# A transformer block's attention on one core: matmuls in column quarters and loop turns of one attention step

## The chip, the cores and the metric

The kernel runs on one core of one Trainium2 chip (trn2). The metric is the device time of one execution in microseconds. The time before is the median of three runs, 1502.8 us (1502.3 to 1504.57).

## What is computed

x has 2 batches of 2048 rows of 256 features, in float32. The block is a feed-forward layer, an attention and the same feed-forward layer again, each added to its input:

```
x = x + 0.5 * ffn(layernorm(x))
x = x + attention(layernorm(x))
x = x + 0.5 * ffn(layernorm(x))

ffn(x):        h = concat([x, -x]) @ K0        K: +1 or -1 by a boolean, 512x1024
               h = 2 relu(s0 h) @ K1           1024x1024
               h = 2 relu(s1 h) @ K2, times s2 1024x256
attention(x):  16 heads of 16 features, q = x wq + bq, k and v alike,
               softmax(q k^T / 4) v, heads side by side, @ wo^T + bo
```

## The kernel before, in words

**Blocks and layers.** The 4096 rows are worked in 8 blocks of 512 for each of the two feed-forwards: u = 0 to 7 is the first, 8 to 15 the second. A layer's output of 128 features for the 512 rows is one bank of PSUM (512 float32 in each of 128 partitions). The first layer (`l1`) and the second (`l2`) have 8 banks per block, the third (`l3`) 2, with rows on the partitions and two tiles of 256 columns in each bank. Activations are held as a float16 value and a float16 rest (`h_hi`, `h_lo`), so each product is made twice. Further kinds of bank are `qk` (q and k of a block), `v`, `out` (output projection) and `sq` (squares of q and k, for a bound on the scores).

**Attention.** There are 32 groups of 4 heads and 512 queries. A group has 8 steps, a step is two tiles of 128 keys. A step has four score pairs: each pair is two products of k with q, one on the lower and one on the upper 64 rows of the array, into two of the four score banks, and one ACTIVATE of ACT (L969) makes `exp` of both, 128x1024, into `prob`. Each tile of keys then has its products with v (`pe_values`, L898 to L915): 4 heads times 2 row halves, each a float32 matmul of 17 columns of weights, at columns 32 j of the array. Such a product stands as two MATMUL records in the trace. `pe_scores` (L880 to L895) makes a score either with all 128 columns of the array in one matmul for each row half, or, when `narrow` is set, as four matmuls of 32 columns (`columns_of`, L815): the same result, in four times as many instructions.

**Side work.** All other matmuls that fall into the time of attention are laid between its steps by a planner that writes one list of steps, `work`, before any instruction is made. Each engine goes through that list and issues its part of it. Side work is laid in pairs of banks (`lay_pair`, L259; `pe_pair`, L820 to L877): one bank on the lower 64 rows, its mate on the upper, and after half of its slots the two change rows, for which PE waits for the semaphore `halves`. A slot is one matmul for each bank, or four for each when `narrow` is set. A pair has 32 slots of 512 columns for `l2` (8 weight tiles, two terms, two row halves) and 8 for `l1`; 64 of 256 columns for `l3`; 4 (float32) for `qk`; 8 of 256 columns (float32) for `v` and `out`. `GAP` says how many slots are laid ahead of each score: 4 for `l1` and `l2`, 8 for `l3`, 1 for `qk`, 2 for `v` and `out`. The banks of a pair (6 and 7) are evicted by DVE and ACT: for `l1` and `l2` DVE makes both parts of one bank (L1007, L1009) and the rest part of the other, ACT (L942) the other's value. The next pair starts when they are free.

**The loop of turns** (L313 to L352). It runs over n = 1, 3, ... 255; one passage, here called a turn, issues the scores 4n to 4n + 7 and the products with v of the tiles 2(n-1) to 2(n-1) + 3, which belong to the steps n - 1 and n. At its head `lay_turn` (L291) lays what is not a pair: steps without matmuls (loads, fetches, `flip`), and long steps of DVE from the waiting list (`norm`, `xn`, `split`, `merge`, `heads`), all of them, or up to a cost of 1.0 where the next pair is of `l2`. If the head of the list `side` is of `l1`, the turn has two halves: two pairs of side slots and scores, then two products with v, each followed by a score; the second half has its side slots and scores in column quarters, the first half at full width. In every other turn four times (side slots, score) come first, all at full width, then four times (product with v, score in quarters). Scores laid behind a product with v are in quarters in every turn. `sq` and `range` are laid between the second and the third product with v (`lay_column`, L299), in such turns only. After the last turn of a group, step `o` lets DVE copy the group's output out of the two banks 4 and 5 (L1142, L1144) and SP store it with 8 DMAs; the next group's first product with v waits for that copy.

**DMAs.** At the first step of a group SP loads the k and q of the group after it (`sp_stage`, L1243 to L1262): 2 DMAs of 512 KB and 2 of 128 KB. It waits for the scores of the group before. SP also stores the output of each group, fetches attention rows, loads x and stores results. The engines' own instructions come over the queues named `instruction`; q8 carries those of PE.

Of the kernel before, what the change touches and what calls it, by code (L numbers as in the profile page):

```python
# [88 lines left out]
def build(nc, x, wq, bq, wk, bk, wv, bv, wo_t, bo, k0, k1, k2, s0, s1, s2, out):  # L89
# [29 lines left out]
    group_steps = key_tiles // 2  # L119
    att_steps = groups * group_steps  # L120
# [12 lines left out]
    def norm_turn(kind, u):  # L133
        steps = [Step("norm", u, kind), Step("xn", u, kind)]
        if kind == 1 or u:
            steps += [Step("split", u, kind), Step("flip", u, kind)]
        return steps

    def turns(kind, u):
        return [Step(kind, u, k) for k in range(kd)]  # L140
# [57 lines left out]
    side = norm_turn(0, 0) + [Step("w0", 0, 0)] + turns("turn_x", 0) + [Step("w0", 0, 1), Step("w0", 0, 2), Step("w1")]  # L198
# [3 lines left out]
    side = [s for s in side if s.kind != "load" or s.u < 2 * blocks]  # L202
# [11 lines left out]
    def lay(s, ring, on_act):  # L214
        s.on_act = on_act
        if s.kind in FILLS:
            numbers.lay(s, ring)
        find[s.kind, s.u, s.m] = s
        work.append(s)
# [10 lines left out]
    GAP = {"l1": 4, "l2": 4, "l3": 8, "qk": 1, "v": 2, "out": 2}  # L230
# [6 lines left out]
    def lay_idle(n):  # L237

        while side and side[0].kind not in GAP:
            s = side.pop(0)  # L240
            if s.kind == "fetch":
                held.append(s)
            elif s.kind in LONG:
                waiting.append(s)
            else:
                lay(s, SHARED, False)
        while held and n > group_steps * (block_groups * (held[0].u - blocks) + 2 * (held[0].m + 1)):
            lay(held.pop(0), SHARED, False)

    def lay_long(most):  # L250

        def unfetched(s):
            return s.kind == "heads" and any((f.u, f.m) <= (s.u, s.m // tpb) for f in held)

        while waiting and LONG[waiting[0].kind] <= most and not unfetched(waiting[0]):
            most -= LONG[waiting[0].kind]
            lay(waiting.pop(0), SHARED, False)

    def lay_pair(slots, narrow=False):  # L259

        s, t = side[0], side[1]
        if not s.n:
            for bank in (s, t):
                bank.on_act = bank is t and t.kind in ("l1", "l2", "qk")
                numbers.lay(bank, SHARED)
                find[bank.kind, bank.u, bank.m] = bank
            s.hi = 0
        lo, s.hi = s.hi, s.hi + slots
        work.append(replace(s, lo=lo, hi=s.hi, n=2 * s.n, mate=t, narrow=narrow))
        if s.hi == 2 * s.n:  # L270
            s.lo, s.hi = 0, s.n
            work.append(replace(t, lo=t.n, hi=t.n))
            del side[0:2]
# [7 lines left out]
    def lay_score(no, narrow=False):  # L281

        n, pair = divmod(no, STEP_BANKS // 2)
        if pair == 0:
            work.append(Step("att", n))
        work.append(Step("score", n, pair, narrow=narrow))

    def lay_values(tile):
        work.append(Step("values", tile // 2, tile % 2))

    def lay_turn(n):  # L291

        lay_idle(n)
        if side[0].kind != "l2":
            lay_long(math.inf)
        else:
            lay_long(1.0)

    def lay_column():  # L299

        if side[0].kind in ("sq", "range"):
            lay(side.pop(0), SHARED, False)

    lay_score(0)
    lay_score(1)
    lay_turn(0)
    lay_pair(5)
    lay_score(2)
    lay_pair(5)
    lay_score(3)  # L310
    lay_pair(6)

    for n in range(1, att_steps, 2):  # L313
        no, tile, whole = 4 * n, 2 * (n - 1), n + 1 < att_steps
        lay_turn(n)
        if side[0].kind == "l1" and whole:
            for _ in range(2):
                lay_pair(4)
                lay_score(no)
                no += 1  # L320
            for _ in range(2):
                lay_values(tile)
                lay_score(no, True)
                no, tile = no + 1, tile + 1
            lay_turn(n)
            for _ in range(2):
                lay_pair(4, True)
                lay_score(no, True)
                no += 1
            for _ in range(2):  # L330
                lay_values(tile)
                lay_score(no, True)
                no, tile = no + 1, tile + 1
        else:
            gap = GAP[side[0].kind]
            for _ in range(4):
                lay_pair(gap)
                lay_score(no)
                no += 1
            if side[0].kind == "l2" and side[0].n:  # L340
                lay_long(1.0)
            for between in range(4):
                lay_values(tile)
                if between == 2:
                    lay_column()
                if whole:
                    lay_score(no, True)
                no, tile = no + 1, tile + 1
        if (n + 1) % group_steps == 0 and whole:
            work.append(Step("o", n // group_steps))  # L350
        if n == group_steps * (groups // 2) - 7:

            assert ("v", blocks - 1, 1) in find
# [1138 lines left out]
```

## Time and profile before

| | |
|---|---|
| median of 3 runs | 1502.8 us |
| profiled execution: its time | 1504.59 us |
| its span in the profile | 1500.6 us |
| PE, matmuls | busy 1489.7 us (99%), 20695 instructions |
| PE, weight loads | busy 667.3 us (44%), 20695 instructions |
| ACT | busy 1154.3 us (77%), 1240 instructions |
| DVE | busy 594.3 us (40%), 1330 instructions |
| POOL | busy 59.6 us (4%) |
| granted TensorE clock | full in all 40 slices |
| chain that ended last | PE 98% |
| first and last start of an attention exp | 269.9 and 1418.0 us |

The profile is of one execution. "Busy" is the time in which at least one instruction of the engine runs; matmuls are pipelined and their ends are modelled, so a busy PE says little of how dense its work is. What a stretch of matmuls costs is read from the starts in the timeline: the time of a group is the start of the next group less its own. In attention the matmuls of one score, side slot group or product with v form one row each. `L873` is the line of all side work, `L894` of the scores, `L914` of the products with v; the shape tells full width (64\*128) from column quarters (64\*32).

### The profile page before, as it was taken

The numbers are of one execution on the slowest core, as the hardware profiler recorded it, in microseconds if no ns is written. First come the engines' busy times: TensorE is split into PE (matmuls) and PEld (weight loads), VectorE is DVE, ScalarE is ACT, GpSimd is POOL, SyncE is SP. The second block draws the span as 40 slices with busy tenths as digits, with TensorE's granted clock in tenths as the row PEclk, the third lists the DMA queues.
The fourth block names the chain that finished last, engine by engine and source line by source line (L and its number), as shares of the span: only waits on it lengthen the run. The fifth ranks groups of instructions, "written<-read, shape, count | busy, mean of one in ns | idle before, by whom it ended". The sixth has DMA issues, their size and how long they took to land.

```text
span 1500.6 us, 46230 instructions
## 1 busy us (share of the span) xinstructions
PE 1489.7 (99%) x20695; PEld 667.3 (44%) x20695; DVE 594.3 (40%) x1330; ACT 1154.3 (77%) x1240; POOL 59.6 (4%) x65
## 2 busy tenths in 40 slices
PE   9999999999999999999999999999999999999999
PEld 4555455434334434443444344344344344344354
DVE  7546755611431353335232332332342341333462
ACT  3221221899999999999999999999999999999821
POOL 2010011001000100010100000000000000000000
PEclk9999999999999999999999999999999999999999
DMA  5121324313221341223223113123111212211010
GB/s 138 45 85 43 85 71 113 86 41 97 69 55 56 98 110 48 71 83 97 83 55 94 45 54 97 41 55 97 41 52 58 83 40 69 91 52 49 23 43 17
DMA packets 110194, 102.40 MB, mean 68 GB/s; under 512 B 55847, under 2 KB 95527, under 8 KB 109991
## 3 DMA queue, kind: packets, MB, share of 16 engines
q1 hardware_dynamic: 109158, 98.60, 23.1%
q8 instruction: 165, 2.70, 0.8%
q10 hardware_dynamic: 832, 0.79, 0.2%
q14 instruction: 39, 0.31, 0.1%
HBM read 61.87 MB, written 25.43 MB: 58 GB/s over the span
## 4 chain that ended last, share of the span: by engine, by line
PE 98%; DVE 1%; DMA 1%; issue 0%; SPq 0%; ACT 0%
PE psum L873 31%; PE psum L914 31%; PE psum L894 15%; PE psum L767 12%; PE psum L779 3%; PE psum L755 3%; PE psum L786 2%; PE psum L799 1%; DMA den_t<-den_rows 0%; DVE den_t L1133 0%; DMA x_sb<-in_x 0%; PE psum L792 0%; DVE stats L1057 0%; DVE xn L999 0%; SPq L1271 0%
## 5 line engine op out<-in xcount | busy, mean ns | idle before, releaser
L969 ACT ACTIVATE prob<-psum 128x1024 f32<-128x1024 f32 x1024 | 1037.7, 1024 | 77.2 <-PE psum L894 30.8
L914 PE MATMUL psum<-prob,v_sb 64*17 64x512 f32 x8192 | 545.3, 591 | 0.0
L894 PE MATMUL psum<-q_st,k_st 64*32 64x512 f16 (+1 forms) x5312 | 411.8, 376 | 0.0
L942 ACT ACTIVATE h_hi<-psum 128x512 f16<-128x512 f32 x183 | 108.3, 597 | 212.7 <-PE psum L767 166.6
L914 PEld LDWEIGHTS psum<-prob,v_sb 64*17 64x17 f32 x8192 | 128.5, 93 | 188.0 <-issue 153.9
L894 PEld LDWEIGHTS psum<-q_st,k_st 64*32 64x32 f16 (+1 forms) x5312 | 121.2, 93 | 202.9 <-ACT prob L969 88.1
L1009 DVE SCALAR_TENSOR_TENSOR h_lo<-psum,h_hi 128x512 f16<-128x512 f32 x256 | 168.1, 687 | 82.9 <-ACT h_hi L942 80.4
L1007 DVE TENSOR_SCALAR h_hi<-psum 128x512 f16<-128x512 f32 x73 | 50.5, 691 | 378.8 <-PE psum L873 378.8
L873 PE MATMUL psum<-h_hi,w 64*128 64x512 f16 x1184 | 152.9, 377 | 1.0 <-issue 0.7
L873 PE MATMUL psum<-h_lo,w 64*128 64x512 f16 x1184 | 152.2, 376 | 0.0
L767 PE MATMUL psum<-h_lo,w 128*128 128x512 f16 x432 | 102.1, 379 | 0.0
L767 PE MATMUL psum<-h_hi,w 128*128 128x512 f16 x432 | 102.1, 379 | 0.0
L873 PEld LDWEIGHTS psum<-h_hi,w 64*128 64x128 f16 x1184 | 52.3, 94 | 98.8 <-issue 41.1
L873 PEld LDWEIGHTS psum<-h_lo,w 64*128 64x128 f16 x1184 | 58.3, 94 | 69.5
L1014 DVE SCALAR_TENSOR_TENSOR x_sb<-psum,scal,x_sb 128x512 f32<-128x512 f32 x32 | 23.2, 748 | 141.8 <-PE psum L873 110.8
L873 PE MATMUL psum<-xn,w 64*32 64x512 f16 (+1 forms) x1440 | 76.0, 378 | 0.2 <-issue 0.2
L1142 DVE COPY o_sb<-psum 128x512 f32<-128x512 f32 x32 | 22.1, 691 | 123.6 <-PE psum L914 123.6
L767 PEld LDWEIGHTS psum<-h_lo,w 128*128 128x128 f16 x432 | 42.2, 98 | 51.2 <-DVE h_lo L1009 0.3
L767 PEld LDWEIGHTS psum<-h_hi,w 128*128 128x128 f16 x432 | 42.2, 98 | 51.2 <-issue 0.9
L1133 DVE RECIPROCAL den_t<-den_t 128x128 f32<-128x128 f32 x64 | 60.5, 945 | 8.5 <-DMA den_t<-den_rows 8.5
L755 PE MATMUL psum<-xn,w 128*128 128x512 f16 x224 | 49.9, 380 | 1.1 <-ACT xn L938 0.9
L873 PEld LDWEIGHTS psum<-xn,w 64*32 64x32 f16 (+1 forms) x1440 | 28.0, 92 | 46.1 <-PE psum L873 13.6
(110 smaller groups left out, 888.1 us busy)
## 6 DMA issues: line engine op xcount, KB each, us to landing
k_st<-k_halves SPq DMA_DIRECT2D x64, 512.0 KB, 4.5
q_halves<-piece SPq DMA_DIRECT2D x32, 256.0 KB, 2.5
q_st<-q_halves SPq DMA_DIRECT2D x64, 128.0 KB, 4.8
x_rows<-x_sb SPq DMA_DIRECT2D x16, 256.0 KB, 2.2
k_halves<-piece SPq DMA_DIRECT2D x16, 256.0 KB, 2.8
att_rows<-o_sb SPq DMA_DIRECT2D x128, 32.0 KB
x_sb<-x_rows SPq DMA_DIRECT2D x8, 512.0 KB, 3.9
att_t<-att_rows SPq DMA_DIRECT2D x16, 256.0 KB
```

The costliest lines, as they stand in the source:

```text
L755: mm = pe.matmul(psum[:, bank, :], w0[:, k, m * P:(m + 1) * P], xt[:, half, k, :], start=(j == 0), stop=(j == s.n - 1))
L767: mm = pe.matmul(psum[:, bank, :], w1[:, k, m * P:(m + 1) * P], (h0_hi, h0_lo)[half][:, k, :], start=(j == 0), stop=(j == s.n - 1))
L779: mm = pe.matmul(psum[:, bank, t * dim:(t + 1) * dim], (h1_hi, h1_lo)[half][:, k, tile * P:(tile + 1) * P], w2[:, k, :], start=(jj == 0), ...
L786: mm = pe.matmul(psum[:, bank, :], w[:, j, half * P:(half + 1) * P], at[:, j, :], start=(j == 0), stop=(j == kd - 1))
L873: mm = pe.matmul(psum[c, bank.bank, wide], w[:, c], a, start=(turned == 0 and j == 0), stop=(turned == 1 and j == length - 1))
L894: mm = pe.matmul(psum[c, SCORES[(h + r) % len(SCORES)], :], k_st[rows, slot, t * P:(t + 1) * P][:, c], q_st[rows, slot, :], start=True, st ...
L914: mm = pe.matmul(psum[32 * j:32 * j + va, O_BANKS[r], :], v_sb[rows, b * key_tiles + t, GROUP * g4 + j, :], prob[rows, h % PROBS, :], star ...
L942: act.activation(hi, psum[:, bank, :], ACT.Relu).then_inc(act_done, 1)
L969: act.activation(prob[:, to:to + 2, :], psum[:, bank:bank + 2, :], ACT.Exp, scale=score_scale / QK_SCALE ** 2).then_inc(exp_sem, 1)
L1007: dve.tensor_scalar(hi[:, m, :], psum[:, bank, :], 0.0, None, ALU.max).then_inc(dve_done, 1)
L1009: dve.scalar_tensor_tensor(lo[:, m, :], psum[:, bank, :], 0.0, hi[:, m, :], ALU.max, ALU.subtract).then_inc(dve_done, 1)
L1133: dve.reciprocal(den_t[:, half, cols], den_t[:, half, cols]).then_inc(den_inv, 1)
```

## The change

The turn in two halves is taken out of the loop and becomes `lay_one_step`, called for n and for n + 1, with side slots and scores all in column quarters. It is used for every turn unless the head of `side` is of `l3` or `v`, or the third entry is `sq`, or it is the last turn. The branch looks at `side` before `lay_turn` has taken from it what is not a pair. The other turns go to `lay_two_steps`, in the order of before (four pairs of side slots and scores, then four products with v and scores), in column quarters as well unless the kind is `l3`. In `lay_turn` the long DVE steps of up to 1.0 are left out where the pair of `l2` has had 24 of its 32 slots, so that with two calls per turn they are laid at 0, 8 and 16 slots.

```
@@ lay_turn
         if side[0].kind != "l2":
             lay_long(math.inf)
-        else:
+        elif side[0].hi < 24:
             lay_long(1.0)
@@ before and in the loop of turns
+    def lay_one_step(n):
+
+        lay_turn(n)
+        gap = GAP[side[0].kind]
+        for pair in range(2):
+            lay_pair(gap, True)
+            lay_score(4 * n + pair, True)
+        for tile in range(2):
+            lay_values(2 * (n - 1) + tile)
+            lay_score(4 * n + 2 + tile, True)
+
+    def lay_two_steps(n):
+
+        lay_turn(n)
+        gap, narrow = GAP[side[0].kind], side[0].kind != "l3"
+        for pair in range(4):
+            lay_pair(gap, narrow)
+            lay_score(4 * n + pair, narrow)
+        if side[0].kind == "l2" and side[0].n:
+            lay_long(1.0)
+        for tile in range(4):
+            lay_values(2 * (n - 1) + tile)
+            if tile == 2:
+                lay_column()
+            if n + 1 < att_steps:
+                lay_score(4 * n + 4 + tile, True)
+
     for n in range(1, att_steps, 2):
-        no, tile, whole = 4 * n, 2 * (n - 1), n + 1 < att_steps
-        lay_turn(n)
-        if side[0].kind == "l1" and whole:
...
-            lay_turn(n)
...
+        if side[0].kind not in ("l3", "v") and side[2].kind != "sq" and n + 1 < att_steps:
+            lay_one_step(n)
+            lay_one_step(n + 1)
         else:
-            gap = GAP[side[0].kind]
...
-        if (n + 1) % group_steps == 0 and whole:
+            lay_two_steps(n)
+        if (n + 1) % group_steps == 0 and n + 1 < att_steps:
             work.append(Step("o", n // group_steps))
```

## Rows read from the trace of the kernel before

**Rows 1.** Windows of one turn each, all engines: busy us (xinstructions), clock, DMA share.
```profile
300.86:309.73 8.87, 8.87 (x144) 3.44 (x138) 0.04 (x1) 8.19 (x9) 0.00 (x0) 1.00 0.30 102
382.00:391.01 9.01, 9.01 (x204) 3.42 (x197) 5.32 (x8) 8.72 (x11) 0.00 (x0) 1.00 0.39 125
354.24:363.33 9.09, 9.09 (x128) 3.33 (x120) 2.16 (x3) 8.50 (x10) 2.04 (x2) 1.00 0.24 79
588.20:597.30 9.10, 9.10 (x144) 4.90 (x136) 1.32 (x3) 8.17 (x9) 0.00 (x0) 1.00 0.31 103
336.33:345.29 8.96, 8.96 (x177) 4.91 (x170) 0.04 (x1) 8.19 (x9) 0.00 (x0) 1.00 0.32 67
```

**Rows 2.** Groups of instructions, shapes kept apart: the full-width score products.
```profile
L894 PE MATMUL psum<-q_st,k_st 64*128 64x512 f16 x960 | 182.6, 376 | 0.0
```

**Rows 3.** Timeline of PE in a second-layer turn: start us, us, work.
```profile
303.90 0.38 PE L894 MATMUL psum<-q_st,k_st 64*128 64x512 f16 x2
304.11 1.03 PE L873 MATMUL psum<-h_lo,w 64*128 64x512 f16 x8
304.98 0.38 PE L894 MATMUL psum<-q_st,k_st 64*128 64x512 f16 x2
305.28 1.08 PE L914 MATMUL psum<-prob,v_sb 64*17 64x512 f32 x16
...
309.38 0.42 PE L894 MATMUL psum<-q_st,k_st 64*32 64x512 f16 x8
309.73 0.39 PE L873 MATMUL psum<-h_hi,w 64*128 64x512 f16 x2
```

**Rows 4.** Timeline of PE in the quarter-width half of a first-layer turn.
```profile
387.33 0.42 PE L894 MATMUL psum<-q_st,k_st 64*32 64x512 f16 x8
387.64 1.06 PE L873 MATMUL psum<-xn,w 64*32 64x512 f16 x32
388.52 0.40 PE L894 MATMUL psum<-q_st,k_st 64*32 64x512 f16 x8
388.74 1.04 PE L914 MATMUL psum<-prob,v_sb 64*17 64x512 f32 x16
```

**Rows 5.** Timeline of DVE in the same half turn: the pair's last evictions.
```profile
389.47 1.29 DVE L1009 SCALAR_TENSOR_TENSOR h_lo<-psum,h_hi 128x512 f16<-128x512 f32 x2
```

**Rows 6.** Timeline of PE around three pauses that no semaphore explains.
```profile
534.32 0.74 PE L894 MATMUL psum<-q_st,k_st 64*32 64x512 f16 x8
534.99 0.39 PE L873 MATMUL psum<-h_hi,w 64*128 64x512 f16 x2
...
926.44 1.04 PE L873 MATMUL psum<-xn,w 64*32 64x512 f16 x28
927.66 0.40 PE L873 MATMUL psum<-xn,w 64*32 64x512 f16 x4 [0.18 <-issue]
...
1287.15 0.41 PE L894 MATMUL psum<-q_st,k_st 64*32 64x512 f16 x8
1288.27 0.39 PE L873 MATMUL psum<-h_hi,w 64*128 64x512 f16 x2 [0.71 <-issue]
```

**Rows 7.** Windows from the start of the span to just before two of the pauses.
```profile
0.00:927.60 927.60, 923.46 (x11991) 418.70 (x11991) 392.55 (x936) 681.55 (x743) 50.11 (x61) 1.00 0.27 76
0.00:1288.20 1288.20, 1283.34 (x18103) 571.31 (x18104) 516.71 (x1177) 1019.36 (x1093) 57.27 (x64) 1.00 0.26 73
```

**Rows 8.** DMA view of the same two windows: the instruction queue.
```profile
q8 instruction: 94, 1.54, 0.7%
...
q8 instruction: 142, 2.33, 0.8%
```

**Rows 9.** DMA view of 285 to 1425 us: the instruction queue.
```profile
q8 instruction: 148, 2.42, 0.9%
```

**Rows 10.** DMA view of 955.9 to 958.6, and of 955.9 to 959.7 us.
```profile
q1 hardware_dynamic: 368, 0.78, 83.9%
...
q8 instruction: 1, 0.02, 1.5%
```

More of the change, by code:

```diff
@@ L311, in build @@
     lay_pair(6)
-    for n in range(1, att_steps, 2):
-        no, tile, whole = 4 * n, 2 * (n - 1), n + 1 < att_steps
-        lay_turn(n)
-        if side[0].kind == "l1" and whole:
[L317 to L324, printed above, removed]
-            lay_turn(n)
[L326 to L333, printed above, removed]
-        else:
-            gap = GAP[side[0].kind]
[L336 to L348, printed above, removed]
-        if (n + 1) % group_steps == 0 and whole:
```

## The prediction, made before the change was run

> **What bounds the kernel now.** I read the windows of single turns first. A turn here is one passage of the loop that the diff replaces: two attention steps and their side work. In all kinds of turn PE is busy for the whole window, 8.87 of 8.87 us in a second-layer turn, while ACT is busy 8.19 [rows 1]. So attention, 128 turns, is paid in PE time. The timeline of PE then shows what the time of a turn is. A full-width score and four side slots repeat every 1.08 us (303.90 to 304.98); four products with v and three quarter-width scores take 4.10 (305.28 to 309.38), and one more score 0.22, so 4 × 1.08 + 4.32 = 8.64; without the rounding about 8.63. The other 0.24 stands at two places: the score before the first product with v lasts 0.30 instead of 0.21, and the last quarter-width score lasts 0.35 instead of 0.22 before the full-width side work [rows 3, 4]. No semaphore is late at either. They are the passages from full-width to column-quarter matmuls and back.
>
> **What a passage removed is worth.** The 960 full-width score matmuls are 480 pairs [rows 2]: 4 ahead of the loop, 2 in each of 18 first-layer turns, 4 in each of 110 others. By the order written in the code these 110 are 73 of the second layer, 18 of the third, 8 of q and k, 7 of the output projection, 4 of v. After the change a turn is wholly in quarters unless it is the wide kind. Of the 18 third-layer turns 15 stay wide. In 3 (blocks 5, 6, 7) the list starts with a merge when the branch looks at it, so the first half of the layer goes to one-step turns in quarters although it is a third layer.
>
> Is a quarter-width side slot as fast? Yes for 512 columns of f16: the 32 matmuls of four quarter slots take 0.88 us (387.64 to 388.52) as the 8 full-width ones take 0.87 [rows 3, 4]. Gains per turn then are:
> second layer 73 × 0.24 = 17.5;
> first layer 18 × 0.19 = 3.4: a pair of blocks changes its row halves after four slots, with only a score between, and in quarters that wait makes the score 0.31 instead of 0.22 [rows 4]. It stands twice per turn, so the turn becomes 8.63 + 0.2 = 8.83 against 9.02;
> q and k 8 × 0.46 = 3.7, and output 7 × 0.47 = 3.3, from 9.09 and 9.10 [rows 1] to 8.63, because the change of halves moves behind two products with v. These are f32 with no quarter-width row; the products with v are also f32 in column tiles and run at the rate of their columns. The bounds are 0.24 and 0.47 a turn, and I take the upper, nearest to that row;
> v 4 × 0.37 = 1.5, as the output but with its change of halves still inside;
> third layer in quarters 3 × 0.33 = 1.0, from 8.96 [rows 1].
> Sum 30.4 us. What hides the rest: exps and evictions stay in their order against scores and pairs, the long DVE steps stay 4.3 us apart, and the staging and store DMAs of SP are the same.
>
> **What becomes tighter.** A pair of blocks now ends some 2.37 us before the next begins (three scores, two products) where the second layer had 4.5. Its evictions end at 389.47 + 1.29 = 390.76, 2.24 after the last side work ended at 388.52 [rows 4, 5]. With 0.12 to spare and a semaphore to pass I bound the stall by 0 and 0.1 us for some 72 pairs, 0 to 7 us, and take 1, as the row is on the safe side. ACT: eight exps of 1.02 and half an eviction of 0.6 are 8.5 of 8.63, and in first-layer turns they overlap (11 instructions, 8.72 busy) [rows 1], so it still waits for PE: nothing.
>
> **What it adds: instructions.** The same work comes in four times as many matmuls and weight loads. A quarter turn holds 256 + 128 + 128 = 512 of them (side, scores, values). The second-layer turn holds 272 now; a third-layer turn in quarters will hold 768. In the trace three pauses stand in the middle of a run of like matmuls, with no wait on anything: the score at 534.32 lasts 0.67 (0.32 over), the side work of 926.44 stops before its last four matmuls until 927.66 (0.37 over), and 1287.15 to 1288.27 is 1.12 (0.77 over) [rows 6]. Between the second and the third PE and its weight loads issued 36207 - 23982 = 12225 instructions, and 48 packets came on the instruction queue [rows 7, 8]: 254.7 each, and 256 with PE's own waits, which the counts leave out; a packet is 2.42 MB / 148 = 16 KB [rows 9]. So the pauses stand at block ends: PE had run out of instructions. One block is 8 us of work in a full-width turn and 4.3 in quarters. A packet can be late: after a staging of k and q, none passed from 955.9 to 958.6 while the data queue took 84% of the engines; it came by 959.7 [rows 10]. At 8 us a block nobody sees that.
>
> The price: all three pauses lie in the quarter halves of first-layer turns, 18 × 4.55 = 82 us in all, and sum to 1.46 us, 1.8%. After the change 102 turns × 8.63 = 880 us have that density: 15.7 us, 14.2 more than now. The three third-layer turns ask for a block every 2.9 us, denser than any row; I bound them by 0 and 10 us (a wait of 1.1 for each of 9 blocks) and take 4, between, as pauses occur already at 4.3. The Trainium skill (Runtime: NRT & Kernel Launch, Instruction fetch mechanics) gives PE 2048 instructions of buffer and calls a block's fetch mostly hidden; by that the 18 us fall away and the sum is 18 lower. The pauses at block ends speak against it here. It also says (TensorE: Matmul & The Clock Gate, Wait — 56ns, not 53.3ns?) that matmuls never start less than about 25 ns apart; by that a quarter slot of the third layer (8 matmuls of 256 columns) takes 0.20 instead of 0.11 us, 9 us more in 96 slots. The trace differs: eight quarter matmuls span 0.39 to 0.42 us where one lasts 0.38.
>
> **Sum.** The profiled execution took 1504.6 us (span 1500.6), 1.8 over the median of 1502.8. 1504.6 - 30.4 + 14.2 + 4 + 1 = 1493.4; against the median 1491.6, so 1492.
>
> **Rivals.**
> A. Instructions cost nothing more (the three pauses were chance, or the buffer copes). For it: three events are few. 1502.8 - 30.4 + 1 = 1473. Chance 0.2. It is where the Trainium skill's page on the runtime, above, would lead.
> B. Slower: the late packet becomes the rule. A staging stands at each of 32 groups, some 27 of them before quarter turns, and lasts as long as a block (955.9 to 958.6 and its own issue before). In quarters every one of them meets a request; in full-width turns many met none. If each costs 1.5 us, that is 40, with 4 for the third layer, 5 for the other bursts and 1 for evictions: 1502.8 - 30.4 + 50 = 1522; at 1.2 us 1514. It decides from about 0.8 us per staging, where 22 + 10 equal the gain. Against it: first-layer quarter halves beside stagings show no pause at most of them. Chance 0.12. A milder form, 0.5 to 0.8 each, ends at 1497 to 1505: chance 0.16.
> C. The passages do not vanish but stay as waits: the evictions or the exps fall due where the passage was. Then second-layer turns keep about 0.1 each, 7 us, and the time is 1499. For it: the 0.12 us of slack. Chance 0.07.
> My forecast, 1484 to 1496, has the remaining 0.45.
>
> **Numbers.** A change under 0.2% (3 us) can't be told from none. Faster by more than that takes in the forecast, A, C in half and a third of the milder B: 0.45 + 0.2 + 0.04 + 0.06 = 0.75. Within: the rest of C and of the milder B, 0.13. Slower: B, 0.12. The range leaves out the low tail of A below 1473 and B above 1508: 1473 to 1508.
>
> **What would show it.** Second-layer turns of 8.62 to 8.65 us where no pause falls, no score longer than 0.23 except in first-layer turns and around the 15 wide turns; full-width score matmuls down from 960 to 128 (15 turns of four pairs, and four pairs at the start); some 60% more PE instructions and some 240 instruction packets from 285 to the end of attention, where 148 were; pauses without a semaphore at block ends, mostly just behind a staging, some 18 to 20 us in sum. I am wrong if the quarter-width f32 or 256-column slots run slower than their columns, if pauses stand elsewhere, or if the sum of pauses is under 5 or over 35 us.

## The result, and the profile of the changed kernel

The changed kernel takes 1507.8 us (median of 11 runs, 1500.2 to 1513.5) against 1502.9 of the kernel before (11 runs, 1502.3 to 1504.7): a ratio of 1.003 [1.0018, 1.0042], slower by 0.3%. The forecast was 1492, in a range of 1473 to 1508, and faster: the time is at the upper end of the range and has moved the other way. The profiled execution took 1509.4, its span is 1505.5. The spread is part of the result: 13 us among runs of the changed kernel, 2.4 among those of before.

The page of the changed kernel: engines, the instruction queue of PE, and the chain that ended last. All line numbers are 3 lower than before (L870 side work, L891 scores, L911 products with v).

```profile
PE 1476.8 (98%) x33079; PEld 780.4 (52%) x33079; DVE 594.6 (39%) x1330; ACT 1151.4 (76%) x1240; POOL 59.8 (4%) x65
...
q8 instruction: 262, 4.29, 1.2%
...
PE 97%; issue 1%; DVE 1%; DMA 1%; ACT 0%; SPq 0%
```

PE has 60% more instructions (20695 before), is busy 12.9 us less in a longer span, and "issue", a wait for nothing that the profile shows, has 1% of the chain that ended last, where it rounded to 0% before.

Scores, shapes kept apart:

```profile
L891 PE MATMUL psum<-q_st,k_st 64*32 64x512 f16 x7680 | 451.1, 376 | 3.5 <-issue 2.8 <-ACT prob L966 0.7
L891 PE MATMUL psum<-q_st,k_st 64*128 64x512 f16 x128 | 24.3, 376 | 0.9 <-ACT prob L966 0.9
```

The full-width scores went from 960 [rows 2] to 128, as the order in the code says. Now windows of single turns, in the columns of [rows 1]: second layer, first layer, q and k, output, third layer in quarters, and a second-layer turn with a pause in it.

```profile
300.43:309.04 8.61, 8.61 (x264) 4.23 (x264) 0.00 (x0) 8.21 (x9) 0.00 (x0) 1.00 0.29 89
519.06:527.91 8.85, 8.85 (x266) 3.50 (x250) 3.96 (x6) 8.68 (x11) 0.00 (x0) 1.00 0.27 80
355.94:364.83 8.89, 8.80 (x200) 3.41 (x188) 2.16 (x3) 8.59 (x10) 1.51 (x2) 1.00 0.02 5
592.10:600.71 8.61, 8.61 (x264) 5.86 (x264) 1.29 (x2) 8.05 (x9) 0.00 (x0) 1.00 0.30 93
472.55:483.15 10.60, 9.29 (x393) 6.26 (x386) 1.07 (x2) 8.32 (x9) 0.00 (x0) 1.00 0.02 5
1071.01:1081.25 10.24, 9.68 (x264) 4.72 (x249) 3.51 (x6) 8.33 (x10) 0.00 (x0) 1.00 0.28 91
```

The fastest turns of these kinds are faster by what was forecast: second layer 8.61 for 8.87, first layer 8.85 for 9.01, output 8.61 for 9.10 [rows 1]. That not all of their kind are, comes below. PE's timeline shows why these are:

```profile
302.37 0.41 PE L891 MATMUL psum<-q_st,k_st 64*32 64x512 f16 x8
302.59 1.05 PE L911 MATMUL psum<-prob,v_sb 64*17 64x512 f32 x16
...
304.52 0.41 PE L891 MATMUL psum<-q_st,k_st 64*32 64x512 f16 x8
304.74 0.63 PE L870 MATMUL psum<-h_lo,w 64*32 64x512 f16 x16
```

The score ahead of the first product with v and the one ahead of side work both last 0.22, where they were 0.30 and 0.35 [rows 3]. The last two windows are the other side. The longest pause in a second-layer turn (a shorter one stands at 310 already), on PE and on the queue of SP:

```profile
565.33 1.06 PE L870 MATMUL psum<-h_hi,w 64*32 64x512 f16 x29
567.84 0.39 PE L870 MATMUL psum<-h_hi,w 64*32 64x512 f16 x3 [1.45 <-issue]
```

```profile
560.20 0.58 SPq L1256 DMA_DIRECT2D k_st<-k_halves  x1
560.83 0.58 SPq L1258 DMA_DIRECT2D q_st<-q_halves  x1
561.46 0.54 SPq L1256 DMA_DIRECT2D k_st<-k_halves  x1
562.04 0.60 SPq L1258 DMA_DIRECT2D q_st<-q_halves  x1
```

PE stops after 29 of 32 like matmuls, with no semaphore in it, just behind a staging. The DMA view of 562.8 to 565.4 has this one queue and no line for q8:

```profile
q1 hardware_dynamic: 246, 0.52, 86.7%
```

The next packet of PE's instructions began only at 565.43 by the trace's DMA records, and PE went on 2.4 us later. That the pauses stand at block ends is seen in windows up to three of them, far apart, with the packets of q8 up to there:

```profile
0.00:475.85 475.85, 466.90 (x7045) 243.94 (x7045) 231.46 (x594) 258.24 (x308) 28.54 (x45) 1.00 0.28 77
0.00:567.80 567.80, 556.27 (x9467) 287.06 (x9467) 264.25 (x663) 342.36 (x395) 34.97 (x50) 1.00 0.29 80
0.00:1358.50 1358.50, 1335.26 (x30899) 706.14 (x30900) 537.32 (x1212) 1076.24 (x1153) 59.78 (x65) 1.00 0.26 73
```

```profile
q8 instruction: 55, 0.90, 0.8%
...
q8 instruction: 74, 1.21, 0.9%
...
q8 instruction: 242, 3.96, 1.2%
```

From the first to the second there are 4844 instructions (9467 + 9467 - 7045 - 7045) and 19 packets, 254.9 each; to the third 42865 and 168, 255.1 each. With PE's own semaphore instructions, which these counts leave out, it is 256: between the first two pauses the trace has 20 of them, and 4864 is 19 times 256.

**Where the time went.** I took the starts of all matmuls in attention, from the second turn to the last. This stretch lasts 1130.0 us before (283.1 to 1413.1) and 1135.5 after (283.2 to 1418.6): +5.5, where the forecast has -11.2. Pauses at block ends (time over the normal distance of two matmuls, some 0.2 us, at the one position in 256 where they all stand) are 26, in sum 23.0 us; before they are 1.6. This count is on the low side: inside a group of matmuls in column tiles most starts are only some 0.002 us apart. Against the median distance at the same place in the order, the gaps at block ends are 29.8 us after and 1.6 before. Half of that, 11.4 us in 14 pauses, lies 4 to 7 us behind a staging, the rest behind fetches of attention rows (`att_t`, `den_t`), loads of x, and in the third-layer turns in quarters. In the waits of 285 to 1425 us the same shows in part, since that view counts only time in which no matmul was still in flight:

```profile
PEld psum L870 <- DVE h_lo L1006: 28.1, 66, 0.8
...
PE psum L870 <- issue: 10.7, 16, 1.5
...
PE psum L911 <- issue: 2.9, 3, 1.9
PE psum L891 <- issue: 2.8, 4, 1.8
```

### The profile page after: what moved, and what is told of

The parts are those of the page before. It is cut to its first block, busy times and chain, and to the rows that moved or that the text cites. A ratio compares the mean times of both kernels' runs of the same rounds, so it can differ in the third digit from the quotient of the medians.

```text
span 1505.5 us, 70998 instructions
## 1 busy us (share of the span) xinstructions
PE 1476.8 (98%) x33079; PEld 780.4 (52%) x33079; DVE 594.6 (39%) x1330; ACT 1151.4 (76%) x1240; POOL 59.8 (4%) x65
## 4 chain that ended last, share of the span: by engine, by line
PE 97%; issue 1%; DVE 1%; DMA 1%; ACT 0%; SPq 0%
PE psum L870 31%; PE psum L911 30%; PE psum L891 15%; PE psum L764 12%; PE psum L776 3%; PE psum L752 3%; PE psum L783 2%; PE psum L796 1%; DMA den_t<-den_rows 0%; DVE den_t L1130 0%; DMA x_sb<-in_x 0%; PE psum L789 0%; ACT prob L966 0%; DVE stats L1054 0%; DVE xn L996 0%
## 5 line engine op out<-in xcount | busy, mean ns | idle before, releaser
L911 PE MATMUL psum<-prob,v_sb 64*17 64x512 f32 x8192 | 559.2, 589 | 2.9 <-issue 2.9
L891 PE MATMUL psum<-q_st,k_st 64*32 64x512 f16 (+1 forms) x7808 | 475.4, 376 | 4.4 <-issue 2.8
L891 PEld LDWEIGHTS psum<-q_st,k_st 64*32 64x32 f16 (+1 forms) x7808 | 157.7, 92 | 192.3 <-ACT prob L966 114.1
L911 PEld LDWEIGHTS psum<-prob,v_sb 64*17 64x17 f32 x8192 | 159.4, 93 | 140.2 <-issue 81.0
L870 PE MATMUL psum<-h_hi,w 64*32 64x512 f16 (+1 forms) x4688 | 163.3, 377 | 5.8 <-issue 5.3
L870 PE MATMUL psum<-h_lo,w 64*32 64x512 f16 (+1 forms) x4688 | 164.7, 376 | 0.0
L870 PEld LDWEIGHTS psum<-h_hi,w 64*32 64x32 f16 (+1 forms) x4688 | 83.6, 92 | 69.0 <-issue 19.1
L870 PEld LDWEIGHTS psum<-h_lo,w 64*32 64x32 f16 (+1 forms) x4688 | 88.3, 93 | 57.9 <-issue 15.1
L870 PE MATMUL psum<-xn,w 64*32 64x512 f16 x2304 | 78.4, 378 | 1.5 <-issue 1.5
L870 PEld LDWEIGHTS psum<-xn,w 64*32 64x32 f16 x2304 | 30.9, 91 | 43.1 <-PE psum L870 14.0
```

Of the source, the lines that this page charges most:

```text
L870: mm = pe.matmul(psum[c, bank.bank, wide], w[:, c], a, start=(turned == 0 and j == 0), stop=(turned == 1 and j == length - 1))
L891: mm = pe.matmul(psum[c, SCORES[(h + r) % len(SCORES)], :], k_st[rows, slot, t * P:(t + 1) * P][:, c], q_st[rows, slot, :], start=True, st ...
L911: mm = pe.matmul(psum[32 * j:32 * j + va, O_BANKS[r], :], v_sb[rows, b * key_tiles + t, GROUP * g4 + j, :], prob[rows, h % PROBS, :], star ...
```

## The experiments

Theory F: the gain of the passages is there, and late instruction blocks behind bursts on the data queue eat it. Rivals: the new order costs it (evictions or exps of the one-step turn; rival W in the expectations), or quarters as such are slow. The pauses below are counted as above, over 0.2 us each, in one profiled execution of each kernel.

**e1: the same bytes, one DMA per step.** The four DMAs of a staging go out at four steps in turn, not all at the first:

```
-                    if s.u % group_steps == 0:
-                        g = s.u // group_steps
-                        if g + 1 < groups:
-                            sp_stage(g + 1)
+                    g, part = divmod(s.u, group_steps)
+                    if part < 4 and g + 1 < groups:
+                        if g and part:
+                            sp.wait_ge(qk_sem, STEP_BANKS // 2 * s.u)
+                        sp_stage(g + 1, part)
```

> The changed kernel, but the four DMAs that load the k and q of the next group (two of 512 KB, two of 128 KB) go out one per attention step, in the first four steps of a group, instead of all four within 2.5 us. Theory F (PE's instruction blocks come late behind bursts of data, and at quarter width a block lasts only 4.3 us): in the profile of the changed kernel 14 pauses at block ends, 11.4 us in all, lie 4 to 7 us behind such a burst; they go or shrink, the time falls by 9 to 15 us, to 1493 to 1499. Rival W (the time went into waits, for evictions and exps, that the shorter distances of one-step turns bring): nothing changes, 1505 to 1511.

Measured 1501.0 (1495.5 to 1505.4), ratio to the kernel before 0.9985 [0.9971, 0.9999] against 1.003 of the changed kernel. Pauses at block ends 16.4 us for 23.0. The direction is as F has it, but the time is above the 1493 to 1499 that I expected: one DMA of 512 KB is a burst still.

**e2: nearly no staging.** From the third group on, the loads of k and q take 2 columns each, so the scores are made from old k and q; all else is as it was.

```
-                sp.dma_start(k_st[:, slot, :], ...
+                whole = slice(0, seq if g < 2 else 2)
+                sp.dma_start(k_st[:, slot, whole], ...
```

> The changed kernel, in which the loads of k and q from the third group on move two columns each instead of 2048 and 512, so that attention goes on with the k and q of the first two groups: the largest bursts of data are gone and nothing of PE, ACT and DVE changes. Theory F: the pauses behind the staging go, 11.4 us and what follows them, to 1490 to 1497. Rival W: 1505 to 1511 as the changed kernel.

Measured 1488.5 (1488.1 to 1489.0), 0.9903 [0.9887, 0.992]. Not one matmul differs from the changed kernel in number or order, and 19 us are gone: the staging's transfers are what costs. Pauses 6.8 us; I put those left down to the other bursts, and e9 tests that. The order is unchanged and the kernel is a little below my range and faster than before, so the order is not what makes the changed kernel slower.

**e3: quarters in turns of two steps.** The branch takes one-step turns for `l1` alone.

```
-        if side[0].kind not in ("l3", "v") and side[2].kind != "sq" and n + 1 < att_steps:
+        if side[0].kind == "l1" and n + 1 < att_steps:
```

> The changed kernel with turns of two steps everywhere but in the first layer, in quarters but for the third layer (all 18 third-layer turns are wide then): evictions have 4.3 us again before the next pair of blocks. Rival W: most of the loss comes back, 1480 to 1490. Theory F: the density of instructions is the same, so the pauses stay; only the three third-layer turns (5 us over their floor) and eviction waits of 0.05 to 0.15 us per pair (5 us) come back: 1497 to 1503, about 1499.

Measured 1505.9 (1499.8 to 1513.4), 1.0022 [1.0002, 1.0042], pauses 18.6 us: the changed kernel within the error of both. The order does not make the loss. It is above the 1497 to 1503 that I had given F, which counted on 10 us from third-layer turns and evictions; its profile still has 18.6 us of pauses with all third-layer turns wide.

**e4: one-step turns, side slots and their scores at full width.**

```
-            lay_pair(gap, True)
-            lay_score(4 * n + pair, True)
+            lay_pair(gap)
+            lay_score(4 * n + pair)
```

> The changed kernel with the side slots and scores ahead of the products with v at full width in one-step turns: the order of the change without its quarters. Each such turn has two passages to quarters and back instead of none. If a passage and its return cost 0.25 us as in the trace of before: some 105 turns at 9.1 us against 8.87, 1525 to 1532. If the passages are cheap and the order is what costs: 1505 to 1512. With few instructions theory F expects no pause at a block's end.

Measured 1526.5, 1.0156 [1.0139, 1.0173]. PE's timeline:

```profile
310.34 0.42 PE L891 MATMUL psum<-q_st,k_st 64*32 64x512 f16 x8
310.69 1.04 PE L870 MATMUL psum<-h_hi,w 64*128 64x512 f16 x8
...
312.64 0.38 PE L891 MATMUL psum<-q_st,k_st 64*128 64x512 f16 x2
312.95 0.65 PE L911 MATMUL psum<-prob,v_sb 64*17 64x512 f32 x8
```

Both passages are back (0.35 and 0.31 for 0.22), twice per turn instead of once, and the pauses are gone (0.6 us): attention takes 1152.3, which is 22.3 over the kernel before, as much as removing one pair of passages per turn gains in e9 below. So the passage is a price of the change of widths, in this order too.

**e6: halves, 64 columns, in place of quarters**, to have half the instructions: `width = P // 2` in `columns_of`.

> The changed kernel with narrow side slots and scores in two column halves of 64 instead of four quarters of 32: half as many added instructions, an instruction block lasts 6 to 7 us; the products with v stay at columns 32 j. Theory F gives nothing for pauses then. If the passage of 0.12 us is between any two column widths, each one-step turn holds four passages: 1522 to 1532. If only full width against column tiles costs a passage, 1474 to 1484.

Measured 1605.4, 1.0681 [1.0663, 1.0699]; I had reckoned with 1522 to 1532. Second-layer turns take 9.70:

```profile
324.96 0.39 PE L891 MATMUL psum<-q_st,k_st 64*64 64x512 f16 x4
325.27 1.07 PE L911 MATMUL psum<-prob,v_sb 64*17 64x512 f32 x16
326.28 0.41 PE L891 MATMUL psum<-q_st,k_st 64*64 64x512 f16 x4
326.62 1.08 PE L911 MATMUL psum<-prob,v_sb 64*17 64x512 f32 x16
327.62 0.41 PE L891 MATMUL psum<-q_st,k_st 64*64 64x512 f16 x4
```

A product lasts 1.01 where it was 0.86, a score behind it 0.34 where it was 0.22. I had counted four passages per turn and forgotten that the scores between products are in halves too: eight, some 0.14 each, 1.09 us per turn. A change between tiles of 64 and of 17 in 32 columns costs a passage too, not only one from full width. The blocks last 7.9 us here and no pause is seen, so the time says nothing of quarters without pauses.

**e11: third layer wide in all 18 turns.** The branch asks for the kind of the next pair instead of the head of the list, and nothing else is changed.

```
-        if side[0].kind not in ("l3", "v") and ...
+        ahead = next(q.kind for q in side if q.kind in GAP)
+        if ahead not in ("l3", "v") and ...
```

> The changed kernel with one edit: the branch looks at the next pair's kind, so that the first halves of the third layer of blocks 5, 6, 7 are wide two-step turns too. In the changed kernel those three turns took 10.17, 10.60 and 10.41 us and the wide ones 8.82 to 8.95; 4.6 us of pauses at block ends lie in them. Theory F: 1500 to 1504, some 5 us less than the changed kernel, as far as the pauses do not move elsewhere with the shifted block ends.

Measured 1504.1 (1502.0 to 1509.7), 1.0018 [1.0005, 1.0032], 3.7 under the changed kernel. The intervals overlap, so the 3.7 is not clear of the noise by itself, but the profile of the changed kernel has what would make it: the three quarter turns last 10.17, 10.60 and 10.41 us, the wide ones 8.82 to 8.95. The timeline of the changed kernel in one of them:

```profile
472.55 1.07 PE L870 MATMUL psum<-w,h_hi 64*32 64x256 f16 x64
473.42 0.41 PE L891 MATMUL psum<-q_st,k_st 64*32 64x512 f16 x8
473.64 0.94 PE L870 MATMUL psum<-w,h_lo 64*32 64x256 f16 x51
475.89 0.40 PE L870 MATMUL psum<-w,h_lo 64*32 64x256 f16 x13 [1.31 <-issue]
```

64 matmuls of 256 columns take 0.87, as 16 at full width; it is the block end in the next group that costs.

**e5: e11 with the staging in small pieces.** Ten DMAs of 128 KB, one for each half step over five steps, each behind the scores of that half step.

```
+                    if part < 5 and g + 1 < groups:
+                        for piece_no in (2 * part, 2 * part + 1):
+                            if g and piece_no:
+                                sp.wait_ge(qk_sem, STEP_BANKS // 2 * s.u + 2 * (piece_no % 2))
+                            sp_stage(g + 1, piece_no)
```

> The changed kernel with two edits: the branch looks at the next pair's kind, so all 18 third-layer turns are wide (the three in quarters ask for an instruction block every 2.9 us and stood 5 to 7 us over the others), and the load of the next group's k and q goes out in ten pieces of 128 KB, one per half step over the first five steps, not in 2.5 us. Theory F: no data burst is long enough to hold an instruction block back for more than the 1.4 us it has to spare at quarter width; the time comes near that of the kernel without staging less the third layer's part: 1480 to 1488. Rival B (a block waits for the sum of the bytes, not for the length of a burst): as one DMA per step, 1495 to 1501, less 6 for the third layer: 1489 to 1495.

Measured 1488.8 (1486.8 to 1494.0), 0.99 [0.9884, 0.9917]: 15.4 under e11, with every byte still moved. Pauses 8.9 us, in the execution of 1494.0. The median is at the border of the two expectations (up to 1488 by F, from 1489 if the sum of the bytes counts) and doesn't decide between them; e9 does.

**e7: the same pieces in the kernel before.**

> The kernel before with the load of the next group's k and q in ten pieces over five steps, as in the run beside it. Theory F: at full width an instruction block lasts 8 us and no burst made PE wait, except in the three pauses of first-layer turns (1.5 us in all): 1501 to 1503, no change that can be told. If the pieces shortened the changed kernel for a reason that has nothing to do with instructions (k and q late, data queue), this one falls as well, by 5 us or more.

Measured 1502.1, 0.9995 [0.9986, 1.0005]: nothing. The pieces help only where blocks run short.

**e8: e5's pieces with e3's order** (two-step turns in quarters).

> Two-step turns in quarters (first layer in one-step turns, third layer wide) with the k and q loads in ten pieces: the order in which evictions have 4.3 us. Theory F: beside the one-step kernel with the same loads it saves the eviction waits, some 4 to 5 us: 1476 to 1484. If the order of two steps costs something of its own, it is above the one-step kernel.

Measured 1492.0 (1490.9 to 1494.2, 4 runs), 0.9931 [0.9915, 0.9948], pauses 10.4 us, 7.5 of them in three places: near 535, 680 and 1046. I had expected 1476 to 1484. It is rather above e5 (1488.8) than below it, so the two-step order does not bring the 4 to 5 us here; with four runs of each I can't say that it costs something.

**e9: e5, and the other bursts calmed too.** x comes in four DMAs for one, and before each of them and each fetch of `att_t` and `den_t` SP waits for one or two further scores.

```
+        def sp_pace(scores):
+            if 0 < pace[0] < STEP_BANKS // 2 * (att_steps - 8):
+                pace[1] = max(pace[0], pace[1] + scores)
+                sp.wait_ge(qk_sem, pace[1])
...
+            for t in range(tpb):
+                sp_pace(1)
+                sp.dma_start(x_sb[:, u % RING, t, :], ...
```

> The kernel with wide third-layer turns and k and q loads in ten pieces, and beside that the loads of x (512 KB) in four pieces and the fetches of attention rows and denominators one by one, each one or two scores behind the one before, where they went out in one burst of five DMAs (1.5 MB). In the profile of the run without this the pauses left at block ends, 8.5 us, stand at 507, 544, 674, 679, 732, 825, 1046 us, nearly all behind that burst. Theory F: they shrink, 1481 to 1486. If pauses remain of the same size elsewhere (chance delays of the instruction queue that no burst makes), 1487 to 1490.

Measured 1481.3 (1480.3 to 1481.3, 4 runs), 0.9853 [0.9836, 0.9869]. This is the best kernel of the study and beats both the kernel before and the changed one. Pauses at block ends are 1.7 us, as before the change, and in the waits of 285 to 1390 us all that is left of PE's issue is (L880 is the side work here):

```profile
PE psum L880 <- issue: 0.3, 1, 0.3
```

Instruction packets and data of that stretch, first in the changed kernel, then in e9:

```profile
q1 hardware_dynamic: 65709, 72.32, 23.1%
q8 instruction: 235, 3.85, 1.4%
```

```profile
q1 hardware_dynamic: 93294, 73.65, 25.8%
q8 instruction: 237, 3.88, 1.4%
```

As many instruction packets, as many bytes, and more packets and more DMA time for the data: neither the number of instructions nor the load of the DMA engines makes the pauses alone; data in one lump in front of a packet that is due does. One thing changed along with the lump: the packets of k are of 4096 bytes in the changed kernel (8192 of them) and of 1024 in e5 and e9 (32768). e1, with packets of 4096 still and the DMAs apart, gained 0.45%; how much of the rest is the shorter lump and how much the smaller packet, no run tells.

**e10: e9's DMAs with e3's order.**

> The same loads in pieces with two-step turns outside the first layer. Theory F and the eviction waits of the one-step order (0.05 us in every other second-layer turn, 0.1 to 0.2 at a layer's end, 4 to 5 us in all) together: 1478 to 1484, 2 to 4 below the one-step kernel beside it. If two steps cost as much in halves waits (q and k, output) as they save, equal within 2 us.

Measured 1482.1, 0.9864 [0.9847, 0.988], the same as e9 within the error. Second-layer turns are 8.61 more often (53 of 71, where e9 has 33 and most of the others at 8.66 to 8.8), output turns 8.78 for 8.61. In sum the second layer has 1.9 us less than in e9, q and k 0.8 less, the output 1.3 more, and the profiled attention is 1.0 shorter: what the one order saves on evictions it gives back in part on the output's changes of row halves. That fits the second expectation, not the 2 to 4 us of the first.

**e12: e9's DMAs in the kernel before.**

> The kernel before with all loads in pieces (k and q, x, attention rows), as in the best kernel so far. Theory F: at full width there is next to nothing to gain, the three pauses of 1.5 us at most: 1500.5 to 1502.5. So of the 21 us between before and the best kernel the pieces alone give at most 2, and the quarters give theirs only with the pieces. If the pieces alone give 5 us or more, theory F has the gain in the wrong place.

Measured 1502.1, 0.9994 [0.9985, 1.0003]: nothing again.

The chain of medians closes: 1507.8, with the third layer wide 1504.1 (-3.7), staging in pieces 1488.8 (-15.4), the other bursts 1481.3 (-7.5). Against e12, which moves its data in the same pieces, the change of widths with the third layer wide is worth 20.8 us. These medians are from different chips; the ratios to the kernel before, taken on the same chip each, say the same (1.003, 1.0018, 0.99, 0.9853).

## Why the prediction was wrong

**Sound: what a passage costs.** The forecast had 8.63 for a second-layer turn, 8.61 measured where nothing is in the way; 8.83 for the first layer, 8.85 in every other turn of e9 and 8.96 in the rest; 8.63 for the output, 8.61; 128 full-width scores; 60% more PE instructions; some 240 instruction packets from 285 us to the end of attention, 243 came. Quarter slots of 256 columns run at the rate of their columns, so the Trainium skill's spacing of about 25 ns (TensorE: Matmul & The Clock Gate, Wait — 56ns, not 53.3ns?) does not hold between matmuls in different column tiles: 64 of them took 0.87 us, 14 ns each.

**Sound: what would be lost.** Pauses without a semaphore, at block ends. The direct sum was forecast at 18 to 20 us and is 23.0, or 29.8 by the median distance; half of it, where the forecast said most, is just behind a staging. Rival A, no pauses, is refuted by e2, e5 and e9; the Trainium skill (Runtime: NRT & Kernel Launch, Instruction fetch mechanics), which calls a block's fetch mostly hidden, agrees nearly with the trace at 8 us a block (1.6 us of pauses before) and not at 4.3 behind a burst. Rival C, waits in place of passages, is refuted by e3 and e10 as the main cause.

**The step that failed is the price of the pauses.** It took 1.46 us of pauses in 82 us of first-layer quarter halves, 1.8%, for the density of 880 us to come. Such a half turn lasts 4.55 us and a block in quarters 4.3, so nearly every block there ran in part through full-width work: by the trace only some 11 of the 148 blocks were used up in under 5.5 us. With 1.46 us over 11 dense blocks the price is 0.13 each, and over 102 × 512 / 256 = 204 such blocks it gives 27 us instead of 15.7. That is rough, for three events carry it, and one of them ended a block of 6.0 us, outside the 11.

Measured, changed kernel less e9: 1135.5 - 1107.7 = 27.8 us, where the forecast had 14.2 and 4 for the third layer. 5.4 of the 27.8 lie in third-layer turns, so that term was about right; the term of 14.2 came to 22.4. The gaps at block ends account for all of it: by the median distance they are 29.8 - 2.2 = 27.6 us more than in e9 (23.0 - 1.7 = 21.3 over 0.2 each), and the 31 turns that hold one are together 29 us longer than their like. In most a turn grows by about its gap. Two second-layer turns grow by clearly more, both with the pause inside products with v: their column tiles get out of step. The turn of the last window above shows it on PE's timeline (from 1074.71 to 1075.86 nothing starts, and the score behind the product starts 0.77 late):

```profile
1074.24 1.05 PE L911 MATMUL psum<-prob,v_sb 64*17 64x512 f32 x11
1075.86 0.61 PE L911 MATMUL psum<-prob,v_sb 64*17 64x512 f32 x3 [0.56 <-issue]
1075.87 0.41 PE L891 MATMUL psum<-q_st,k_st 64*32 64x512 f16 x5
1076.10 0.40 PE L870 MATMUL psum<-h_lo,w 64*32 64x512 f16 x5
...
1080.74 0.68 PE L891 MATMUL psum<-q_st,k_st 64*32 64x512 f16 x8
```

Product, score and side slots, issued one after the other, are mixed in their starts for 5 us, and the turn is 10.24 long, 1.6 over its like, for a gap of 1.15; the other (gap 1.0 at 1111) is 10.23.

**A term mis-sized: the gain.** Attention in e9 against before is 1130.0 - 1107.7 = 22.3 us, 22.4 with the pauses (1.6 and 1.7) left out of both, where the passages were put at 30.4 less 1 for evictions. By kinds, sums of all turns before less those of e9, the forecast in brackets: second layer 630.0 - 617.7 = 12.3 (17.5), first layer 164.1 - 160.4 = 3.7 (3.4), q and k 72.7 - 71.3 = 1.4 (3.7), output 63.8 - 60.3 = 3.5 (3.3), v 37.8 - 37.7 = 0.1 (1.5), third layer, wide here, 161.5 - 160.3 = 1.3 (1.0). The first layer's 3.7 holds some 1.6 of pauses that e9 doesn't have: its passages gave 2.1. So the second layer, q and k, v and the first layer are all short.

The evictions were put at 1, between bounds of 0 and 7. The second layer's own turns in e9 are at 8.61 and 8.66 in turn, mostly 8.75 to 8.9 at the end of a layer, in sum 6.4 over 71 × 8.61. In many of them PE waits for the last pair's eviction. DVE and PE of the changed kernel:

```profile
334.22 1.29 DVE L1006 SCALAR_TENSOR_TENSOR h_lo<-psum,h_hi 128x512 f16<-128x512 f32 x2
...
335.39 0.56 PE L891 MATMUL psum<-q_st,k_st 64*32 64x512 f16 x8
...
335.85 0.41 PE L870 MATMUL psum<-w,h_hi 64*32 64x256 f16 x16
```

The eviction ends at 335.51, the weight load follows at 335.82, and the score between lasts 0.46 for 0.22. In the waits of attention, weight loads wait 28.1 us for `h_lo` in 66 cases (view above), before 15.1 in 34. The order of e10, which gives evictions two products more time, brings this back: in the waits of 285 to 1390 us, weight loads wait 15.2 us for `h_lo` in 36 cases in e10 and 30.1 in 70 in e9.

Leaving out turns with a pause, the second layer is 5.5 us over 8.61 a turn in e9 and 2.6 in e10. So about 3 us go with the one-step order, to the evictions by these waits, and 2.6 stay in either order, with a cause that no run looked into. The slack of 0.12 that the forecast read off [rows 5] was real, but not enough for the semaphore and the layer ends: 3 us, within the bounds of 0 and 7, where 1 was taken.

q and k turns came to 8.88 to 8.93 instead of 8.63: I had taken the gain of the moved change of halves in full, the upper of two bounds, and 0.25 to 0.3 of its 0.46 is not there. Why the output turns reached the bound while q, k and v did not, no run looked into.

**The sum by measured terms:** 1130.0 - 22.3 + 27.8 = 1135.5, which closes by its making, since both terms are differences to e9. The forecast in the same terms was 1130.0 - 29.4 + 18.2 = 1118.8: of the 16.7 us between, 9.6 are the pauses and 7.1 the gain. The 15.4 us that e5 took off e11 are 0.57 for each of the some 27 stagings ahead of quarter turns: the milder form of rival B, which the forecast put at 0.5 to 0.8 for each, 1497 to 1505 in all, and a chance of 0.16. Its price was right; its time was not, because the gain beside it was smaller, and so it ends on the slow side. That the time of 1507.8 is still inside the range is no merit of the sum.

## What to carry to other kernels

Matmuls in column tiles of one width save the passages between widths, 0.24 us for each pair of them here, but they multiply the instructions. What follows is an estimate from the two block times of this case, 4.3 and 8 us, and was not tried at others. Before such a change, divide the time of a dense turn by its instructions per 256 (4.3 us a block here) and set it beside the longest lump on the data queues (2.5 to 3 us, with a packet's 2.4 us to take effect behind it); if the two together exceed the block, as here (and not at 8 us), split the transfers into pieces of some 128 KB and pace them by work done, in the same change. That did nothing for the kernel before (e7, e12) and, with the third layer wide throughout, turned this change from +0.3% into -1.5%.

## What the runs showed of the hardware that was not expected

- Two column widths both narrower than the array still cost a passage: 0.12 to 0.15 us for each change between tiles of 64 and tiles of 17 in 32 columns (e6).
- After a pause within products with v in column tiles the tiles stay out of step for some 5 us, and the turns grew by 1.6 us for gaps of 1.15 and 1.0 (two cases, at 1075 and 1111); in most other turns the growth is about the gap.
- A kernel whose instruction blocks run short varies from run to run: 13 us among the runs of the changed kernel and 14 in e3 (10 or 11 runs), about 1 in e2 and e9 with the same or nearly the same instructions (4 runs each). e5, with more pauses than these and fewer than the changed kernel, has 7 in 4 runs.
- Open: whether a packet is held back behind a lump by the order in each DMA engine or by the memory, and whether the length of the lump or the size of its packets decides; no run tells them apart.
